# One block for a chunk's normalization, turning and projections, with the experts' sums in it; head halves first; stores awaited in the attention

## What is computed

```python
x = x + conv_attention_0(ln(x, 1e-6))      # c0: qkv, 12 heads of 16, scores * 0.25 + rel_h + rel_w, softmax, projection
t = t + routed_experts(ln(t, 1e-5))        # f0: 8 experts of 384, the best 2 of each token, silu(a) * u
x = x + conv_attention_1(ln(x, 1e-6))      # c1: as c0 with its own weights
t = f1(ln(x))                              # ln, attention without positions, MLP of 768, 4 gated experts of 768
```

## Time and profile before

| | us |
|---|---|
| median of 3 runs (3319.51 to 3328.25) | 3325.3 |
| the profiled execution | 3325.34 |
| its span | 3323.8 |
| c0: normalization, projections, position products and stores, attention's first instruction | from 16.8, 47.3, 117, 178.5 |
| c1: gathers, normalization, projections, position products, attention's first instruction | from 1103.4, 1198.9, 1229.3, 1298, 1359.3 |
| f1: two normalizations, projections, last product's values, attention's first instruction | from 1960.4, 2017.7, 2068.2, 2104.8 |

### The profile page before, as it was taken

How to read it: one execution, slowest core, us unless ns; L and a number is a source line. 1 busy time by engine, 2 the same in 40 slices (tenths; PEclk the granted TensorE clock), 3 DMA queues, 4 the chain that set the end, 5 groups by cost and what they waited for, 6 DMA issues and landing times. The chain is left out here.

```text
span 3323.8 us, 62798 instructions
## 1 busy us (share of the span) xinstructions
PE 2587.4 (78%) x18516; PEld 1200.4 (36%) x18516; DVE 2460.0 (74%) x4648; ACT 1861.5 (56%) x2594; POOL 502.0 (15%) x559
## 2 busy tenths in 40 slices
PE   4749999997499227389999956188888859499998
PEld 2512222226499215122222233011111147266666
DVE  6878999975755348689999855599999645465665
ACT  3526777782255116167777736077777825555554
POOL 1210211111333523101111100101111100000000
PEclk9859999996699659599999977599999979699999
DMA  2575677754122213766666601112122110200000
GB/s 59 188 144 112 143 143 149 151 116 145 34 78 77 69 30 136 172 118 151 142 141 149 145 17 55 55 41 62 57 62 62 48 32 1 71 6 5 9 5 14
DMA packets 208983, 281.99 MB, mean 85 GB/s; under 512 B 56606, under 2 KB 100366, under 8 KB 208842
## 3 DMA queue, kind: packets, MB, share of 16 engines
q1 hardware_dynamic: 169258, 216.05, 28.0%
q0 software_dynamic: 19920, 31.57, 4.0%
q10 hardware_dynamic: 19664, 32.60, 3.3%
HBM read 201.65 MB, written 77.46 MB: 84 GB/s over the span
## 5 line engine op out<-in xcount | busy, mean ns | idle before, releaser
L804 DVE TENSOR_REDUCE c0att_mx<-c0att_m 128x1 f32<-128x512 f32 x768 | 493.4, 685 | 34.0 <-PE c0att_m L741 28.7
L804 DVE TENSOR_REDUCE c1att_mx<-c1att_m 128x1 f32<-128x512 f32 x768 | 493.5, 685 | 32.1 <-PE c1att_m L741 27.0
L804 DVE TENSOR_REDUCE f1att_mx<-f1att_m 128x1 f32<-128x512 f32 x768 | 480.1, 682 | 21.1 <-PE f1att_m L741 18.9
L1053 ACT ACTIVATE c0att_p<-c0att_s 128x1024 f32<-128x1024 f32 x384 | 373.9, 1020 | 150.1 <-PE c0att_s L757 150.0
L1053 ACT ACTIVATE c1att_p<-c1att_s 128x1024 f32<-128x1024 f32 x384 | 373.9, 1020 | 148.6 <-PE c1att_s L757 148.5
L1053 ACT ACTIVATE f1att_p<-f1att_s 128x1024 f32<-128x1024 f32 x384 | 373.2, 1020 | 121.3 <-PE f1att_s L757 121.3
L741 PE MATMUL f1att_m<-f1att_km,f1att_qm 48*128 48x512 f16 x768 | 156.3, 402 | 155.6 <-DVE f1att_mx L804 99.6
L1483 ACT ACTIVATE moe_h<-moe_u,moe_bu 128x512 f32<-128x512 f32 x192 | 136.5, 711 | 175.9 <-PE moe_u L1400 93.8
L770 PE MATMUL c0att_o<-c0att_p,c0att_vs 128*32 128x512 f32 x1536 | 206.3, 609 | 0.6 <-ACT c0att_p L1053 0.6
L741 PE MATMUL c1att_m<-c1att_km,c1att_qm 64*128 64x512 f16 x768 | 156.1, 402 | 64.5 <-DVE c1att_mx L804 34.9
L770 PE MATMUL f1att_o<-f1att_p,f1att_vs 128*32 128x512 f32 x1536 | 205.6, 607 | 0.7 <-ACT f1att_p L1053 0.5
(11 more groups left out here) (623 smaller groups left out, 5323.9 us busy)
## 6 DMA issues: line engine op xcount, KB each, us to landing
xt<-rel_parts SPq DMA_DIRECT2D x256, 128.0 KB, 5.1
xt<-qk_parts SPq DMA_DIRECT2D x192, 128.0 KB, 4.4
y<-rel_parts SPq DMA_DIRECT2D x128, 128.0 KB, 5.2
y<-qk_parts SPq DMA_DIRECT2D x96, 128.0 KB, 4.7
c0att_qm<-rel_parts SPq DMA_DIRECT2D x144, 64.0 KB, 2.1
c1att_qm<-rel_parts SPq DMA_DIRECT2D x144, 64.0 KB, 2.1
f1att_ka<-qk_parts SPq DMA_DIRECT2D x144, 64.0 KB, 2.1
expert_rows<-y SPq DMA_DIRECT2D x39, 192.0 KB, 2.0
```

Of the source, the lines that this page charges most:

```text
L804: dve.tensor_reduce(mx[:, n:n + 1], bank[:, :], AX.X, ALU.max).then_inc(s_mx, 1)
L1053: act.activation(pr[h][kt % 2][:, :], sps[h][:, :], ACT.Exp).then_inc(s_e, 1)
```

## The change

A new function `front` takes the place of `start`, `layer_norm` and `qkv` for c0, c1 and f1. In it:
- all engines work a chunk at a time through normalization, transposes, parts and projections; each list interleaves chunk c with c - 1. For c0 it loads x (weights and constants behind or beside it), for c1 it gathers and adds the experts' rows chunk by chunk (ring of four chunks), for f1 it does the inner normalization per two chunks. ScalarE normalizes in c1 and f1, VectorE in c0;
- the scale of the queries goes into the weights, the bias becomes a sixth matmul of each group, so that ScalarE writes each group once and VectorE takes the low part from PSUM;
- the copies into column order (high and low) are all ScalarE's;
- projections use three banks each for groups and values, one pair for transposes, position products all eight;
- in f1 GpSimd's queue stores the keys, SP's the queries; the stage doesn't wait for stores to land.

`attention` waits for the stores itself (`projected`, `stored`) and takes the pairs of heads 0 to 5 of all batches first, then those of heads 6 to 11 (`place`). `layer_norm` keeps only the form that the last block uses. `routed_experts` ends after its last store.

```diff
+def front(nc, name, src, eps, stats, parts, ident, vt, w, scratch, kept, spare=None, load=None, back=None, hidden=None):
...
+    SET = TC if back else 2 * TC
+    by_act = load is None
...
+        t0, t1 = m.ps("t0"), m.ps("t1")
+        qp = [m.ps(f"qp{u}") for u in range(3)]
+        vp = [m.ps(f"vp{u}") for u in range(3)]
+        rp = qp + vp + [t0, t1]
...
+                            store_qk(sp, b, g, s, kept["qk"][g])
...
+                def gather(c):
+                    if c >= LAG:
+                        pool.wait_ge(s_add, 2 * TC * (c - LAG + 1))
+                    for k in range(2):
+                        for j in range(TC):
+                            t = c * TC + j
+                            pool.indirect_dma_start(
+                                ring[c % LAG][k][:, j * C:(j + 1) * C], None, scratch["yd"][:, :],
+                                bass.IndirectOffsetOnAxis(back["give"][:, k * TILES + t:k * TILES + t + 1], 0)
+                                ).then_inc(back["sems"][c], 16)
+                if back:
+                    gather(0)
...
+                if back:
+                    for c in range(1, CHUNKS):
+                        gather(c)
...
+                    for b in range(B):
+                        for g in range(GROUPS):
+                            pool.wait_ge(s_lo, (2 * b + 1) * GROUPS + g + 1)
+                            store_qk(pool, b, g, 1, kept["keys"])
...
+                def turn_over(c):
+                    pe.wait_ge(s_norm, TC * (c + 1))
+                    if c:
+                        pe.wait_ge(s_xlo, 2 * c)
+                    for j in range(TC):
+                        pe.transpose(t0[:, j * P:(j + 1) * P], nrm[c % 2][:, j * C:j * C + C0], ident)
+                        ins = pe.transpose(t1[0:C1, j * P:(j + 1) * P], nrm[c % 2][:, j * C + C0:(j + 1) * C], ident)
+                    ins.then_inc(s_turned, 1)
...
+                    if g == 0:
+                        pe.wait_ge(s_xlo, 2 * c + 2)
+                    if n >= 3:
+                        pe.wait_ge(s_lo, n - 2)
+                    bank = qp[n % 3][:, :]
...
-                    pe.matmul(bank, bl[:, wide], xb[:, cols], start=False, stop=True).then_inc(s_qk, 1)
+                    pe.matmul(bank, bl[:, wide], xb[:, cols], start=False, stop=False)
+                    pe.matmul(bank, cl[:, wide], ones[:, :], start=False, stop=True).then_inc(s_qk, 1)
...
+                for c in range(CHUNKS + 1):
+                    if c == 1:
+                        pe.wait_ge(s_wl, 3)
+                        pe.wait_ge(s_wh, 4)
+                        pe.wait_ge(s_zero, 2)
+                    if c:
+                        for g in range(2):
+                            turned(c - 1, g)
+                            values(TC * (c - 1) + g)
+                    if c < CHUNKS:
+                        turn_over(c)
+                    if c:
+                        turned(c - 1, 2)
+                        for j in range(2, TC):
+                            values(TC * (c - 1) + j)
...
+                            if n >= 8:
+                                pe.wait_ge(s_rlo, n - 7)
...
+                def prepare(c):
+                    if back:
+                        dve.wait_ge(back["sems"][c], 16 * 2 * TC)
+                        for k in range(2):
+                            if k:
+                                dve.wait_ge(s_add, 2 * TC * c + TC)
+                            for j in range(TC):
+                                t = TC * c + j
+                                cols = slice(t * C, (t + 1) * C)
+                                dve.scalar_tensor_tensor(out=src[:, cols], in0=ring[c % LAG][k][:, j * C:(j + 1) * C],
+                                                         scalar=back["top"][:, k * TILES + t:k * TILES + t + 1],
+                                                         in1=src[:, cols], op0=ALU.mult, op1=ALU.add).then_inc(s_add, 1)
+                        dve.wait_ge(s_add, 2 * TC * (c + 1))
+                    if TC * c % SET:
+                        return
+                    tiles = range(TC * c, TC * c + SET)
+                    if load:
+                        dve.wait_ge(s_x[c // 2], 16)
+                    if hidden:
+                        for t in tiles:
+                            dve.tensor_scalar(src[:, ts(t, C)], hidden["x"][:, ts(t, C)], mean0[:, t:t + 1],
+                                              rstd0[:, t:t + 1], ALU.subtract, ALU.mult).then_inc(s_inner, 1)
+                        dve.wait_ge(s_inner, TC * c + SET)
+                    for t in tiles:
+                        dve.bn_stats(stats[:, ts(t, 6)], src[:, ts(t, C)]).then_inc(s_stats, 1)
+                    dve.wait_ge(s_stats, TC * c + SET)
+                    spread(TC * c, SET, mean, TC * c // SET + sets)
...
+                def finish(c):
+                    if TC * c % SET == 0:
+                        settle(TC * c, SET, mean, rstd, TC * c // SET + sets)
+                    if by_act:
+                        return
+                    dve.wait_ge(s_rstd, 5 * (TC * c // SET + sets + 1))
+                    if c >= 2:
+                        dve.wait_ge(s_turned, c - 1)
+                    for j in range(TC):
+                        t = TC * c + j
+                        dve.tensor_scalar(nrm[c % 2][:, j * C:(j + 1) * C], src[:, ts(t, C)], mean[:, t:t + 1],
+                                          rstd[:, t:t + 1], ALU.subtract, ALU.mult).then_inc(s_norm, 1)
...
+                def low_parts(c):
...
+                    dve.tensor_tensor(xa_lo[:, cols], upper, xa_hi[:, cols], ALU.subtract).then_inc(s_xlo, 1)
+                    dve.tensor_tensor(xb[C1:P, cols], under[0:C1, :], xb[0:C1, cols], ALU.subtract).then_inc(s_xlo, 1)
+                def take(c):
+                    for j in range(TC):
+                        t = TC * c + j
+                        b, kt = t // KT, t % KT
+                        if j < GROUPS:
+                            n, cols = c * GROUPS + j, at(c, j)
+                            dve.wait_ge(s_hi, n + 1)
+                            dve.scalar_tensor_tensor(out=low[:, cols], in0=qp[n % 3][:, :], scalar=1.0 / W_SCALE,
+                                                     in1=high[:, cols], op0=ALU.mult, op1=ALU.subtract).then_inc(s_lo, 1)
...
+                if hidden:
+                    spread(0, TILES, mean0, 0)
+                    settle(0, TILES, mean0, rstd0, 0)
+                    dve.wait_ge(s_rstd, 5)
+                else:
+                    if load:
+                        prepare(0)
+                dve.wait_ge(s_w, 7 * 16)
+                for t in (raw_a, raw_b, raw_c):
+                    dve.tensor_scalar(queries_of(t), queries_of(t), float(HD) ** -0.5, None, ALU.mult).then_inc(s_q, 1)
+                if not load:
+                    prepare(0)
+                finish(0)
...
+                for c in range(CHUNKS + 1):
+                    if c:
+                        take(c - 1)
+                    if c < CHUNKS:
+                        low_parts(c)
+                    if c + 1 < CHUNKS:
+                        prepare(c + 1)
+                        finish(c + 1)
...
+                def normalize(c):
+                    if TC * c % SET == 0:
+                        root(TC * c, SET, TC * c // SET + sets)
+                    if not by_act:
+                        return
+                    act.wait_ge(s_rstd, 5 * (TC * c // SET + sets + 1))
+                    if c >= 2:
+                        act.wait_ge(s_turned, c - 1)
+                    for j in range(TC):
+                        t = TC * c + j
+                        act.activation(nrm[c % 2][:, j * C:(j + 1) * C], src[:, ts(t, C)], ACT.Identity,
+                                       bias=away[:, t:t + 1], scale=rstd[:, t:t + 1]).then_inc(s_norm, 1)
...
+                def high_parts(c):
+                    cols = slice(c * CHUNK, (c + 1) * CHUNK)
+                    act.wait_ge(s_turned, c + 1)
...
+                            act.activation(out[0:n, cols], tile[0:n, :], ACT.Identity).then_inc(s_xhi, 1)
...
+                def high_of(c, g):
+                    n = c * GROUPS + g
+                    act.wait_ge(s_qk, n + 1)
+                    act.activation(high[:, at(c, g)], qp[n % 3][:, :], ACT.Identity,
+                                   scale=1.0 / W_SCALE).then_inc(s_hi, 1)
+                def by_column(c):
+                    act.wait_ge(s_v, TC * (c + 1))
+                    act.wait_ge(s_lo, GROUPS * (c + 1))
+                    act.wait_ge(s_hi, GROUPS * (c + 1))
+                    for g in range(GROUPS):
+                        for rows, buf in ((slice(0, GW), high), (slice(GW, P), low)):
+                            act.activation(by_columns(by_x[g][rows, :], c), by_rows(buf, c, g),
+                                           ACT.Identity).then_inc(s_byx, 1)
...
```

(50 more changed lines are left out.)

448 lines of the change are left out of this document (196 added, 252 removed).

## The result

The changed kernel takes 3265.2 us (median of 4 runs, 3259.7 to 3268.6) against 3324.3 before (4 runs, 3319.5 to 3328.3); the ratio is 0.982, with an interval of 0.980 to 0.984. Forecast was 3248, with a range of 3203 to 3303. The profiled execution took 3268.6 (span 3266.5), the sum had given 3248.3 for it: 20 us too few.

The account below looks back on a forecast made before the run. No engine is full ahead of the attentions; the stages are chains of round trips and queues. Savings of 6 (c0) + 60 (c1) + 11 (f1) = 77 us from 3325.3 give 3248 us, range 3203 to 3303.

Parts of the forecast that it names:

- The overlap with the gathers: c1: gathers, eight of 1.25 us a chunk, hidden behind periods of 13.5 or more; c1 with the landing 60 us less.
- The three loops: Seven chunk periods each: c0 80 us with two periods at 1.2 GHz, c1 103, f1 100.
- R: Moment at which the position products can start: forecast 113 in c0 (117 before), 1240 in c1 (1298 before).
- The reordered pairs: Attentions: pair order by halves of the heads keeps every load, sum and store at its size; 0, between -5 and +10.
- the rule that the prediction names for them: Rival in c1: GpSimd can't write descriptors while VectorE holds the shared port pair in two-port mode; towards 3287 us, chance 0.07.
- The high clock: Rival: TensorE's clock high throughout the fronts of c0, c1, f1; -9, -10, -11 us, 3218 us; chance 0.22.
- the low one: Rival: clock low throughout all fronts, position products too; +28, +11, +11, +14 us, 3312 us; chance 0.11.
- No ScalarE copy of this form is in the trace; 0.58 is the like-sized one from PSUM: c0, after the last product: twelve column-order copies on ScalarE at 0.58 us each, ending 7 us after position products can start.
- The bound of 1.47: Slow-copies rival, c0 and c1: ScalarE's copies at GpSimd's 1.47 us lengthen only the ends, 22 us: 3270; slow copies 0.06.
- The turning point of 1.5 us: Beyond it ScalarE's column copies set c0's and c1's period, each further us costing 108 us; half of slow copies' 0.06.
- issue ends some 2.4 us after the last product, border 2: f1's end: two queues with 24 stores each over 100 us; attention at 2094 against 2104.8, 11 us less.
- the 36 us tail: f1 before the change: SP issues 48 stores at a median of 1.16 us, leaving 36 us with no engine at work.

## Why the prediction was right, and where it was not

**Right**: faster, by c1. The overlap with the gathers was put at 60 us and gave 58; taking it away costs 68. The three loops came within some 4 us of their sums, R within 3. In c0 that is luck in part: no period was as short as the 9.0 forecast for the high clock (9.5 to 14.7), and what they were longer by is about what I had added for two at 1.2 GHz. The reordered pairs cost 0, as put; the gathers ran beside VectorE at 0.95 to 1.13 us and held up nothing (the rule that the prediction names for them speaks of VectorE's two-port modes; no run shows that the sums use one). The high clock did not come (0.75 to 0.86), the low one neither. The granted clock of 1.00 in the first two rows should not have been read as one: no level is recorded there ahead of 60 us, and 64 transposes take the same 15.48 us as in f1's row at 0.50. At the high level eight take 0.93 us in the changed kernel (65.21 to 66.14), where I had put 1.05.

**c0, 5 us of the 20, and 5 more in c1**: the step "No ScalarE copy of this form is in the trace; 0.58 is the like-sized one from PSUM". It is 1.12. The bound of 1.47 covered it: 12 copies, 13.5 us in place of 7, put the first low store at R + 17. In c0 R was 1 us late too and the border 1 us longer than put, and the 48 stores, at 43.4 us in place of 45.4, gave 2 back. In c1 the same 5 us are hidden in the sum, because R came 3 us early: luck, not a right price. The turning point of 1.5 us was wrong for c0: with 6.7 us of copies ScalarE's own 9.6 us a chunk already equal the shortest periods, and the root behind the copies cost 1.1 us twice. In c1, with its longer periods, the copies do stay hidden. The like-sized row differed in where it reads (PSUM against SBUF) and in its pattern of rows and columns; which of the two makes the price was not tried.

**f1, 11 us of the 20**: the step "issue ends some 2.4 us after the last product, border 2". The issue did, at 1.7. What failed is that I read the median of 1.16 us in the earlier trace rows as SP's own work in issuing, where it was the pace at which the DMA engines, at a share of 0.2, took 128 KB in that form: with the layout alone the same issue takes 0.6 us. So I put the landing behind the last issue at nothing beyond the border of 2; it is 12.4 us from the last product to the attention where I had 4.4. The view to read was there: a DMA share of 0.24 beside a queue that never ran dry was a narrow transfer, not a busy SP. The other 3 us are the 1.7 of f1's beginning and 1.3 of loop and last product.

**A deeper error that no number of the forecast shows**: I took the 36 us tail for part of what merging removes. The run with the layout alone removed it from the kernel before; what was left of merging in f1 was a loss of 18 to 23 us. A sum of savings against a stage that waits for something else credits the edit with the wait.

**The last 3 us**: c1's 2 are the 5 of the copies less the 3 of R, and 1 us in the last attention and what follows is within what these vary (1217 to 1221 us in all runs). **The two us of the awaited stores** ("The stage no longer waits for the last landing: 2 us less") came out as 0.9: the border behind the last issue is 3.0 and was 3.9.

Open: why f1's loop takes 94.6 us in some executions of the same code and 100.4 in others (the granted clock is higher in the short one of the keys' run, 0.76 to 0.93 by stretch, than in the long one of the changed kernel, 0.69 to 0.82, but nothing shows what sets it); and why the run with the keys on ScalarE has a ratio 0.003 above the changed kernel's, when its profiled execution, the fastest of its five, shows no loss. c0's loop varies in the same way, from 80.5 to 84.6 us with the same code, and moves R with it (113.3 to 118.2); single profiles of c0 are good to some 4 us. c0 apart was not tried; its merged form reaches the attention at 168.9 to 172.4 us (the three runs with layout and VectorE's copies), the kernel before with the layout at 174.2, so merging bought some 2 to 5 us there.

## What to carry to other kernels

Merging stages into one loop of dependent steps pays what it overlaps with something long (here the gathers, 58 us), and costs a round trip per chunk; where nothing long is beside it, two stages that each keep an engine busy were about 20 us faster. Before crediting an edit with an idle tail, look at what the DMA engines do in it: a share of 0.2 at 100 GB/s with a full queue meant that the outer dimension of the store (four heads) was too small, and one change of layout was worth 37 us in the kernel before. Work put on an engine that is free in the loop still stands at its end, and ahead of whatever that engine has to do next in its list: divide the last pieces among the engines that are idle there.

## What the runs showed of the hardware

- Stores of 64 rows x 2 KB to four heads of 16: 105 GB/s at a DMA share of 0.2, on one hardware queue or two, mostly four packets under way at a time; with GpSimd's queue beside SP's up to 232 GB/s; the same bytes as one block of 64 rows: up to 328 GB/s at 0.9.
- GpSimd copying in SBUF stops VectorE's operations with two SBUF inputs for a copy's length (0.16 to 1.06 us, eight sums from 2.85 to 6.14) and slows its f16 copies of one SBUF tile (0.61 to 1.55), but not its statistics or its operations with an operand in PSUM; GpSimd's gathers leave the sums alone.
- A copy of 64x512 f16 that turns rows into columns: 1.12 us on ScalarE, 0.55 on VectorE, 1.1 on GpSimd (12 in 13.34).
- More matmuls in TensorE's idle time (51 us busy of 63, 86 of 110, 85 of 116) left the granted clock between its levels (0.92, 0.84, 0.83).
